# Attention: query and key parts brought to their stacked, zero-padded rows by transfers within SBUF

## The reference, cut to what matters

```python
B, L, D, H = (32, 64, 512, 32)     # names in the setup; x here is (2, 512, 512), HD = 16
q = (x @ Wq.T + bq).reshape(b, l, h, hd).transpose(0, 2, 1, 3)
k = (x @ Wk.T + bk).reshape(b, l, h, hd).transpose(0, 2, 1, 3)
v = (x @ Wv.T + bv).reshape(b, l, h, hd).transpose(0, 2, 1, 3)
scores = jnp.einsum('bhqd,bhkd->bhqk', q, k) / math.sqrt(hd)
scores = jnp.where(causal, scores, -jnp.inf)
att = jax.nn.softmax(scores, axis=-1)
out = jnp.einsum('bhqk,bhkd->bhqd', att, v)
return out.transpose(0, 2, 1, 3).reshape(b, l, d) @ Wo.T + bo
```

## Time and profile before

| | us |
|---|---|
| median of 3 runs (1709.1 to 1710.33) | 1710.32 |
| the profiled execution, device time | 1712.04 |
| its span (first to last instruction) | 1710.3 |
| mean granted TensorE clock, as a share of full speed | 0.962 |
| PE busy over the span | 1549.1 (91%) |
| DVE, ACT, POOL busy over the span | 1222.2, 826.1, 945.8 |
| from the first scores of the loop to the last | 1233.7 to 1511.7 |

### The profile page before, as it was taken

How to read it: one execution, slowest core, us unless ns; L and a number is a source line. 1 busy time by engine, 2 the same in 40 slices (tenths; PEclk the granted TensorE clock), 3 DMA queues, 4 the chain that set the end, 5 groups by cost and what they waited for, 6 DMA issues and landing times.

```text
span 1710.3 us, 26565 instructions
## 1 busy us (share of the span) xinstructions
PE 1549.1 (91%) x8870; PEld 1215.7 (71%) x8870; DVE 1222.2 (71%) x2024; ACT 826.1 (48%) x1639; POOL 945.8 (55%) x861
## 2 busy tenths in 40 slices
PE   5899999999999999999999879996899999987791
PEld 3677877878778778778787657874567767666681
DVE  5778788778778787877887866567466677767525
ACT  3464554554555545455554423331276666663231
POOL 4367576676675766776756851007442344327544
PEclk9999999999999999999999889998899999997796
DMA  3111012021110110211101111221000000032435
GB/s 119 38 50 59 17 50 64 12 79 38 48 61 18 49 61 12 80 37 49 61 19 50 56 56 62 74 99 37 1 14 1 14 1 1 28 146 75 133 133 166
DMA packets 49498, 92.61 MB, mean 54 GB/s; under 512 B 8016, under 2 KB 32720, under 8 KB 44176
## 3 DMA queue, kind: packets, MB, share of 16 engines
q1 hardware_dynamic: 45744, 79.58, 14.4%
q0 software_dynamic: 3680, 12.06, 2.1%
HBM read 81.14 MB, written 10.49 MB: 54 GB/s over the span
## 4 chain that ended last, share of the span: by engine, by line
PE 59%; DVE 17%; POOL 8%; issue 7%; ACT 6%; DMA 3%; SPq 0%; POOLq 0%; DVEq 0%; ACTq 0%
PE banks L360 28%; PE banks L1666 6%; DVE tap L1237 4%; PE banks L1943 3%; PE banks L1803 3%; PE banks L1731 2%; PE banks L1908 2%; PE banks L1725 2%; PE banks L1696 2%; DMA x<-in_w_gate 2%; PE banks L1933 2%; POOL wol L365 2%; PE banks L1740 2%; DVE xbc L1243 1%; DVE acc L629 1%
## 5 line engine op out<-in xcount | busy, mean ns | idle before, releaser
L1237 DVE SCALAR_TENSOR_TENSOR tap<-banks,parg,tap 128x511 f32<-128x511 f32 (+2 forms) x288 | 215.0, 747 | 26.9 <-ACT tap L943 19.6
L723 POOL TENSOR_TENSOR am<-ah,upto 128x1024 fp32r<-128x1024 f32 x64 | 121.6, 1901 | 179.7 <-PE banks L1696 138.6
L874 POOL TENSOR_SCALAR kz<-kst,head 128x512 fp32r<-128x512 f32 x64 | 99.0, 1564 | 160.3 <-DVE kst L1493 160.3
L360 PE MATMUL banks<-xTh,wch 128*128 128x512 f32 x384 | 162.8, 424 | 5.2 <-DVE em L1343 3.7
L951 ACT ACTIVATE th<-tap 128x512 f32<-128x512 f32 x96 | 60.7, 632 | 215.0 <-DVE tap L1237 212.9
L360 PE MATMUL banks<-xTh,wcl 128*128 128x512 f32 x384 | 151.2, 394 | 0.0
L360 PE MATMUL banks<-xTl,wch 128*128 128x512 f32 x384 | 150.7, 393 | 0.0
L1169 ACT ACTIVATE prob<-banks,nmax 128x128 f32<-128x128 f32 (+3 forms) x256 | 121.6, 529 | 55.3 <-DVE nmax L1504 55.1
L1504 DVE TENSOR_REDUCE nmax<-banks 128x2 f32<-128x256 f32 (+3 forms) x128 | 104.7, 818 | 40.5 <-PE banks L1934 40.3
L723 POOL TENSOR_TENSOR am<-al,upto 128x1024 fp32r<-128x1024 f32 x64 | 122.1, 1908 | 0.0
L1343 DVE TENSOR_TENSOR em<-banks,gmask 128x1024 f32<-128x1024 f32 x64 | 78.2, 1221 | 49.8 <-ACT banks L992 48.9
(11 more groups left out here) (290 smaller groups left out, 4393.1 us busy)
## 6 DMA issues: line engine op xcount, KB each, us to landing
x<-grownT SPq DMA_DIRECT2D x96, 128.0 KB, 4.8
x<-in_w_conv SPq DMA_DIRECT2D x7, 1536.0 KB, 6.5
x<-in_w_gate SPq DMA_DIRECT2D x8, 1024.0 KB, 4.9
x<-in_w_out SPq DMA_DIRECT2D x8, 1024.0 KB, 4.8
eraw<-in_expert_w SPq DMA_DIRECT2D x8, 1024.0 KB, 7.3
gur<-in_ff_gu SPq DMA_DIRECT2D x7, 1024.0 KB, 4.7
x<-in_hidden SPq DMA_DIRECT2D x16, 256.0 KB, 3.6
mates<-yd SPq DMA_DIRECT2D x8, 512.0 KB, 4.6
```

Of the source, the lines that this page charges most:

```text
L360: m = nc.tensor.matmul(o, a, b, start=first and n == 0, stop=last and n == len(terms) - 1)
L723: m = pool.tensor_tensor(am[:, part, :, :], a[:, i, :].bitcast(F32).unsqueeze(2).to_broadcast([P, HG, P]), upto[:, :].unsqueeze(1).to_broa ...
L874: m = pool.tensor_scalar(kz[:, quad % 2, p2, j, :], kst[:, p2, :].bitcast(F32), head[:, j:j + 1], None, ALU.mult)
L1237: nc.vector.scalar_tensor_tensor(tap[:, q % 2, sh:L], bk(CONV_BANKS[q % 2])[:, 0:L - sh], parg[:, KC * q + k:KC * q + k + 1], tap[:, q % 2 ...
```

## The change

The stacks are gone. SP copies rows of `qh` and `ql` from SBUF to SBUF, straight to their places in `qs` and `kz`. The layout becomes three blocks of 32 rows: high, low, high of the queries against high, high, low of the keys; rows 96 to 127 stay zero, and so do the rows of the other head in `kz`, both set once by POOL ahead of the loop. A quad takes 6 transfers of 32 rows (64 KB) for `qs` and 12 of 16 rows (32 KB) for `kz`, 18 in all, 288 in the kernel. The factor 1/4 is put on the query weights and the query bias by ACT. The pieces are now quarters of a projection (3 matmuls), at s = 3, 4, 5, 6 for queries and s = 8, 9, 10, 11 for keys.

```diff
-            for at, what in ((0, ("k", 0, 1)), (1, ("k", 1, 1)), (2, ("q", 0, 1)), (3, ("q", 1, 1))):
-                if s == at:
-                    return (m,) + what
-            for at, what in ((5, ("proj", 0, 0)), (6, ("proj", 0, 1)), (8, ("proj", 1, 0)), (9, ("proj", 1, 1)),
-                             (11, ("k", 0, 0)), (12, ("k", 1, 0)), (13, ("q", 0, 0)), (14, ("q", 1, 0))):
-                if s == at and m + 1 < AT * NB:
-                    return (m + 1,) + what
+            for w, at in ((0, (3, 4, 5, 6)), (1, (8, 9, 10, 11))):
+                if s in at and m + 1 < AT * NB:
+                    return m + 1, w, at.index(s)
...
+        STACK = 2 * (3 + 3 * 2)
+        def stacked(quad):
+            return 16 * STACK * (quad // 2 + 1)
...
+                for m in range(AT * NB):
+                    for u in range(2):
+                        quad = 2 * m + u
+                        if quad >= 2:
+                            sp.wait_ge(s_ready, 8 * (quad - 1))
+                        for w in range(2):
+                            sp.wait_ge(qk_l, 2 * m + w + 1)
+                            for p2 in range(2):
+                                of = 32 * (2 * u + p2)
+                                for r, part in enumerate((qh, ql, qh) if w == 0 else (qh, qh, ql)):
+                                    if w == 0:
+                                        sp.dma_start(qs[32 * r:32 * r + 32, quad % 2, p2, :].bitcast(F32), part[of:of + 32, w, :].bitcast(F32)
+                                                     ).then_inc(qk_in[quad % 2], 16)
+                                    else:
+                                        for j in range(2):
+                                            row, at = of + HD * j, 32 * r + HD * j
+                                            sp.dma_start(kz[at:at + HD, quad % 2, p2, j, :].bitcast(F32), part[row:row + HD, w, :].bitcast(F32)
+                                                         ).then_inc(qk_in[quad % 2], 16)
+                    t = m // NB
+                    if m % NB == 0 and t + 1 < AT:
+                        sp.wait_ge(aq_lo, 2 * t + 2)
+                        sp.dma_start(aqr[:, 0, :, :], wq[t + 1]).then_inc(aq_in, 16)
+                        sp.dma_start(aqr[:, 1, :, :], wk[t + 1]).then_inc(aq_in, 16)
...
-                sp.wait_ge(st_ps, 4 * QUADS)
+                for n in range(2):
+                    sp.wait_ge(qk_in[n], stacked(QUADS - 2 + n))
...
+                    made(pool.memset(kz[:, :, :, :, :].bitcast(F32), 0.0))
...
+                pool.memset(qs[3 * 32:P, :, :, :].bitcast(F32), 0.0).then_inc(sel_ready, 1)
...
-                def padded(quad, p2):
-                    pool.wait_ge(st_k, 2 * quad + p2 + 1)
...
+                    nc.scalar.activation(aqr[:, 0, :, :], aqr[:, 0, :, :], ACT.Copy, scale=HD ** -0.5).then_inc(q_scaled, 1)
+                    act.wait_ge(q_scaled, t + 1 + (t > 0))
...
                 def high(m, w):
                     act.wait_ge(qk_ps, 2 * m + w + 1)
+                    if m:
+                        for u in range(2):
+                            act.wait_ge(qk_in[u], stacked(2 * (m - 1) + u))
...
-                def queries(quad, p2):
-                    act.wait_ge(st_ps, 4 * quad + 2 + p2 + 1)
...
+                nc.scalar.activation(abqk[:, 0, :], abqk[:, 0, :], ACT.Copy, scale=HD ** -0.5).then_inc(q_scaled, 1)
...
-                def keys(quad, p2):
-                    dve.wait_ge(st_ps, 4 * quad + p2 + 1)
...
-                    mat(bk(7), selz[:, pr, 2 * w, :], qh[:, w, :], start=True, stop=False)
-                    mat(bk(7), selz[:, pr, 2 * w + 1, :], ql[:, w, :], start=False, stop=True).then_inc(st_ps, 1)
...
                         if n % 8 == 0:
-                            pe.wait_ge(kpad, 2 * quad + 2)
-                            pe.wait_ge(st_q, 2 * quad + 2)
+                            pe.wait_ge(qk_in[quad % 2], stacked(quad))
```

More of the change, by code:

```diff
@@ L180, in program @@
         osb = sc("osb", [P, L])
-        kst = sc("kst", [P, 2, L], F32R)
+        under_qs = sc("under_qs", [P, 2, L])
         qs = sc("qs", [P, 2, 2, L], F32R)
@@ L866, in _ @@
                     low(pool, awl[:, k, :], awr[:, k, :], awh[:, k, :]).then_inc(aw_lo, 1)
-                def padded(quad, p2):
-                    pool.wait_ge(st_k, 2 * quad + p2 + 1)
-                    if quad >= 2:
-                        pool.wait_ge(s_ready, 8 * (quad - 1))
-                    for j in range(2):
-                        m = pool.tensor_scalar(kz[:, quad % 2, p2, j, :], kst[:, p2, :].bitcast(F32), head[:, j:j + 1],
-                                               None, ALU.mult)
-                    m.then_inc(kpad, 1)
-                for p2 in range(2):
-                    padded(0, p2)
                 for n in range(UNITS):
-                    piece = pieces(n)
-                    if piece and piece[1] == "k":
-                        padded(2 * piece[0] + piece[3], piece[2])
                     if n % 32 == 14 and n // 32 + 1 < AT:
@@ L1173, in _ @@
                         if piece:
-                            m, what, i, u = piece
-                            if what == "proj" and u == 1:
-                                high(m, i)
-                            if what == "q":
-                                queries(2 * m + u, i)
+                            m, w, part = piece
+                            if part == KT - 1:
+                                high(m, w)
                         if n % 32 == 14 and n // 32 + 1 < AT:
@@ L1486, in lows @@
                                                    qh[:, w, :].bitcast(F32), ALU.add, ALU.subtract).then_inc(qk_l, 1)
-                def keys(quad, p2):
-                    dve.wait_ge(st_ps, 4 * quad + p2 + 1)
-                    if quad >= 1:
-                        dve.wait_ge(kpad, 2 * quad - 1 + p2)
-                    nc.vector.tensor_copy(kst[:, p2, :], bk(7)).then_inc(st_k, 1)
                 for w in range(2):
                     lows(0, w)
-                for p2 in range(2):
-                    keys(0, p2)
                 for n in range(UNITS + O_BACK - 7):
@@ L1535, in _ @@
                     if piece:
-                        m, what, i, u = piece
-                        if what == "proj" and u == 1:
-                            lows(m, i)
-                        if what == "k":
-                            keys(2 * m + u, i)
+                        m, w, part = piece
+                        if part == KT - 1:
+                            lows(m, w)
                 dve.wait_ge(wide_in, 32)
@@ L1873, in project @@
                     o = products(bk(7), [(aqh[:, w, k, :], aql[:, w, k, :], xTh[:, k, tok], xTl[:, k, tok])
-                                         for k in (2 * part, 2 * part + 1)], first=part == 0, last=part == 1)
-                    if part == 1:
+                                         for k in (part,)], first=part == 0, last=part == KT - 1)
+                    if part == KT - 1:
                         o.then_inc(qk_ps, 1)
-                def stack(m, what, p2, u):
-                    n, w, pr = ORDER.index((what, p2)), "qk".index(what), 2 * u + p2
-                    if n == 0:
-                        pe.wait_ge(qk_l, 2 * m + 2) if u == 0 else pe.wait_ge(st_q, 4 * m + 2)
-                    elif n < 3:
-                        pe.wait_ge(st_k, 4 * m + 2 * u + n)
-                    else:
-                        pe.wait_ge(st_q, 4 * m + 2 * u + 1)
-                    mat(bk(7), selz[:, pr, 2 * w, :], qh[:, w, :], start=True, stop=False)
-                    mat(bk(7), selz[:, pr, 2 * w + 1, :], ql[:, w, :], start=False, stop=True).then_inc(st_ps, 1)
-                def prepare(m, what, i, u):
-                    if what == "proj":
-                        project(m, i, u)
-                    else:
-                        stack(m, what, i, u)
                 def weighted(quad, hf):
@@ L1914, in _ @@
                 for w in range(2):
-                    for part in range(2):
+                    for part in range(KT):
                         project(0, w, part)
-                for what, i in ORDER:
-                    stack(0, what, i, 0)
                 pe.wait_ge(v_f, NT)
-                pe.wait_ge(sel_ready, SEL + 2)
+                pe.wait_ge(sel_ready, SEL + 3)
                 for n in range(UNITS + O_BACK - 7):
@@ L1957, in _ @@
                     if piece:
[L1958 removed]
+                        project(*piece)
                 for i in range(NT + 6):
```

46 lines of the change are left out of this document (9 added, 37 removed).

## The result

The changed kernel takes 1722.72 us (median of 4 runs, 1721.38 to 1725.35) against 1709.72 us beside it: 1.0085 times, interval 1.0072 to 1.0097. It is slower, by 13 us. The time lies in the range of 8 in 10 (1682 to 1726) and outside the forecast's own (1690 to 1703); the direction was forecast wrong.

A forecast was written before the change was run, and what follows sets the result against it. PE was taken to bound the attention loop. Six steady periods x 1.6 (35.8 to 34.2), first period 1.3, start 1.1 and end 2.0 sum to 14.0 us, forecast 1696.5; own range 1690 to 1703, 8 in 10 1682 to 1726.

The forecast's parts named there:

- `high` waits for nothing: ACT in round 6: the second quad's transfers land about 8 us into the period, needed 13 us in, so no wait.
- Landing: Step 4 of the key-transfer wait before round 16: the last transfer lands 2.0 us after its issue, floor 1.0.
- The gain behind the last transfer: Last 16 rounds of the loop: no projection and no wait for one, so 4 stacks go whole, 2.0 us gained.
- one after another: Rival: transfers do not overlap, 36 of 2 us and more per period, 72 us against 36, over 1950; chance 0.02.
- the slower rival: Rival: SP issues 0.70 apart, period 36.95, 1718; with half clock behind the waits 1738; middle 1726; chance 0.28.
- step 1: Key-transfer wait: PE ends round 11 24.8 us after a period's first scores, from 27.0 less four stacks of 0.55.
- step 3 of the new wait: Before round 16: SP issues 12 key transfers 0.45 apart, the last 4.95 us after the first.
- the rival with 5.8 us of idle time: The slower rival: at 0.70 per issue PE idles 5.8 us before round 16 and may restart at half clock; chance 0.28.
- step 2: Key-transfer wait: `qh`, then `ql`, are done 2.4 us after PE's end of round 11.
- PE alone at 31.2: Steady 16-round period if nothing else waits: 35.8 falls to 31.2 us, by 4.4 for stacks and 0.2 of waiting.
- At the ends: Loop start gains 1.1 us (7.0 from keys' `ql` to first scores, against 8.07), first period 1.3, last rounds 2.0.

The follow-up runs named there:

- `probes`: Changed kernel without transfers after the first projection's, plus 8 test transfers at each of seven places; issue 0.60 us within SBUF, 0.42 to 0.43 from memory; no kernel time given.
- `keep_clock`: Changed kernel with 12 unused matmuls on PE ahead of the first scores of every 16 rounds; 1716.17 us, ratio 1.0032 to the kernel before.
- `keys_first`: Changed kernel with the two projections swapped, keys at s = 3 to 6 and queries at 8 to 11; 1696.85 us, ratio 0.9928.
- `two_of_three`: Changed kernel without the third block of 32 rows, so 4 query and 8 key transfers per quad and one product missing; 1697.02 us, one run.
- The four kernels with halves: Changed kernel with projections in halves at the old rounds: without later transfers 1690.23, with all 1691.81, keys first and retimed 1685.78, that with GpSimd issuing some key transfers 1683.9.

## Why the prediction was wrong

**Right.** No stack is left, PE waits 3.0 us ahead of rounds 16, 32, ... for the keys' last transfer, nothing waits ahead of rounds 8, 24, ..., and `high` waits for nothing. Landing is 2.0. `qh` and `ql` are done 2.2 after PE's end of round 11 (1295.70 to 1297.91), predicted 2.4. The gain behind the last transfer was to be 2.0 and is 1.5 (27.25 to 25.74). A quad's transfers overlap, the last one ending the wait 2.0 after its issue, so the rival "one after another" is out. And the slower rival was named, with its point of decision at a spacing of 0.60; that the time lies near its middle of 1726 is in part luck. With 0.63 its own sum gives a period of 36.2 and 1712, and it charged the clock to 5.8 us of idle time; what filled the rest was the clock behind 3.0 us and the error of step 1.

**Wrong, step 3 of the new wait: the spacing.** 0.63, predicted 0.45: the last of 12 goes out 6.87 after the first instead of 4.95, 1.9 us a period. I chose "two-dimensional loads" as the nearest rows and held against the rival that these transfers have neither a broadcast nor a fourth dimension. The `probes` show that it matters where the two ends are, and no row of the kernel before had both in SBUF.

**Wrong, the clock.** I took it that an idle stretch of 3.0 keeps the clock, since one of 3.49 had the earlier trace rows, and charged it only to the rival with 5.8 us of idle time. After waits of 2.96 to 3.21 us PE ran at a granted 0.50 five times of five, 1.2 us each by `keep_clock`. And the row that I relied on is no rule: the same matmul of the feed-forward block, which no version changes, starts after 3.46 to 3.49 us of idle time in all 14 traces, and behind it the granted clock is 1.00 in 5 of them and 0.50 in 9. Here are the changed kernel, then `keys_first`, each row with the window behind it.

```profile
1168.28 0.50 PE L1778 MATMUL banks<-dn,hidh 128*128 128x512 f32 x1 [3.48 <-DVE hidl L362]
1168.28:1171.28 3.00, 3.00 (x13) 2.45 (x14) 1.85 (x5) 0.00 (x0) 1.64 (x2) 1.00 0.00 0
...
1167.36 0.80 PE L1779 MATMUL banks<-dn,hidh 128*128 128x512 f32 x1 [3.47 <-DVE hidl L362]
1167.36:1170.36 3.00, 3.00 (x7) 2.42 (x8) 1.85 (x5) 0.00 (x0) 1.64 (x2) 0.50 0.00 0
```

One trace had shown me one of two outcomes. The terms of a period add up: 34.2 + 1.9 (spacing) + 1.2 (clock) + 0.5 (the rest of step 1) - 0.2 (step 2) is 37.6, and a period is 37.6 to 37.8.

**Wrong, step 1 and PE alone at 31.2.** PE's end of round 11 came 26.5 after the first scores (1269.17 to 1295.70), not 24.8; 1.2 of that is the half clock. And PE was ready for the next ones after 34.7 (1269.17 to 1303.84), not 31.2: 1.2 by the clock, the rest by the quarters and by what 96% of busy time had hidden, of which only a part shows as waits for the vector and scalar engines. So the measured wait is as long as the predicted one only because both its ends moved: the transfers landed 3.5 later than I said (37.7 for 34.2) and PE came 3.5 later. The 3.0 us that I saw PE ahead were really less than one. This error alone would not have turned the forecast: without the half clock (1.2) and with a spacing of 0.45 (1.9) the period of 37.7 would be near 34.6, beside the 34.40 that `two_of_three` reached with 2.5 us of issues less. That is worked out, not measured; the spacing and the clock behind it made the difference between faster and slower.

**At the ends.** The start lost 0.9 instead of gaining 1.1: `ql` of the keys ends at 1224.17 and the first scores start at 1233.16, 9.0 us where 8.07 stood before and 7.0 were predicted, by the same 1.9 of spacing. The first period lost 1.3 instead of gaining 1.3, 2.6 in all: the spacing is 1.9 of that, and the loop's first rounds ran longer at a granted 0.50 than before, up to 1241.7, 8.5 us in, against 1239.8, 6.1 us in.

**Sum by periods.** Six steady periods cost 6 x (37.91 - 35.83) = 12.5 where 9.6 were to be gained, the first 1.3, and the rest gave 1.5: 12.3, the loop's difference.

## What to carry to other kernels

When a chain of small transfers replaces work, count the issues between the last producer and the first consumer, and take the price of one from a row with the same two ends; the order of producers (keys first) or a second issuing engine can be worth more than any of the bytes. A PE that is busy 96% of a stage may still be held by the other engines as soon as its own work shrinks: before a removed operation is booked in full, see which wait comes out behind it, round by round. And a wait of a few us on PE costs more than its own length, where the clock falls behind it; one row in which it did not fall doesn't settle that, so look at the same place in several traces.

## What the runs showed of the chip

- In a close row an issue on SP of a transfer within SBUF takes 0.58 to 0.60 us and of one from memory to SBUF 0.42 to 0.43, whether of 16 or 128 rows. The first of a row within SBUF takes 0.51 to 0.54 in the loop of the changed kernel, and a load right behind such a row still takes 0.58 (`aqr<-in_wq`, three of three; the load behind it 0.43). On GpSimd an issue within SBUF takes 0.48.
- Idle time alone doesn't tell what the clock does. Here are stretches of the changed kernel: two behind PE's wait of 3.21 us; two behind the wait of 3.81, where the clock fell only at 1460.1, 0.9 us after PE had started again; one behind no wait above 1.09; and one behind the wait of 1.49, at 1.00.

```profile
1419.80:1422.80 3.00, 3.00 (x15) 2.71 (x15) 0.51 (x2) 0.94 (x3) 0.09 (x1) 0.50 0.40 98
1422.80:1425.80 3.00, 3.00 (x17) 2.72 (x16) 1.61 (x3) 1.51 (x4) 0.00 (x0) 0.50 0.25 59
1459.25:1462.25 3.00, 3.00 (x18) 2.73 (x19) 1.15 (x3) 1.22 (x3) 0.00 (x0) 0.65 0.40 98
1460.50:1463.50 3.00, 3.00 (x17) 2.81 (x16) 1.12 (x2) 1.65 (x4) 0.00 (x0) 0.50 0.36 87
1490.90:1494.20 3.30, 3.30 (x25) 2.00 (x24) 2.02 (x3) 2.66 (x5) 0.00 (x0) 0.50 0.21 50
...
1497.07:1500.07 3.00, 3.00 (x26) 2.74 (x27) 1.45 (x3) 1.94 (x5) 0.00 (x0) 1.00 0.40 98
```

- Stretches at half clock behind no long wait, as the one at 1490.9, stand in the loops of five of the kernels with quarters; in `keys_first` 1432.1 to 1435.5, after a stretch in which PE was busy 2.5 of 3.9 us. The four kernels with halves have none. What brought them about wasn't tested.
